# Half of the weight-stream loads issued from ScalarE's queue, and the two stores of x_out released one by one, in a four-sublayer hybrid layer on 8 cores

## The reference

```python
x = x + _L0_attn_a_ref(_layernorm(x), ...)   # S4: causal convolution of length 4096 along the last axis, plus D*u
x = x + _L0_ffn_ref(_layernorm(x), ...)      # (xf * in_scale) @ sign(weight).T * out_scale + bias
x = x + _L0_attn_b_ref(_layernorm(x), ...)   # qkv projection, attention over the 2 sequences, output projection
x = x + _L0_ffn_ref(_layernorm(x), ...)      # the same ffn again
```

## Time and profile before

| | us |
|---|---|
| three runs | 9665.15, 9514.95, 9159.04 (median 9514.95) |
| profiled execution, its own time | 9171.16 |
| span of its slowest core (core 1) | 9169.6 |
| TensorE matmul busy | 5810.7 (63%) |
| TensorE weight loads busy (beside the matmuls) | 2509.5 (27%) |
| VectorE busy | 1786.8 (19%) |
| ScalarE busy | 1271.6 (14%) |
| GpSimd busy | 62.7 (1%) |

### The profile page before, as it was taken

How to read it: one execution, slowest core, us unless ns; L and a number is a source line. 1 busy time by engine, 2 the same in 40 slices (tenths; PEclk the granted TensorE clock), 3 DMA queues, 4 the chain that set the end, 5 groups by cost and what they waited for, 6 DMA issues and landing times.

```text
span 9169.6 us, 74755 instructions; the slowest of 8 cores (9125.0 to 9169.6 us)
## 1 busy us (share of the span) xinstructions
PE 5810.7 (63%) x25740; PEld 2509.5 (27%) x25740; DVE 1786.8 (19%) x3462; ACT 1271.6 (14%) x2520; POOL 62.7 (1%) x108
## 2 busy tenths in 40 slices
PE   2402444566777747775686668774777568767876
PEld 0101111122333323332333233332333223323332
DVE  3212010022211222121202221122112131212112
ACT  0211000011111121111111111112111121111111
POOL 0000000000000000000000000000000000000000
PEclk9855676777788768887787778876887778777887
DMA  1299999955266505663464526650665346452664
GB/s 45 69 263 184 160 154 159 184 155 184 63 211 208 179 37 184 211 187 116 147 220 147 183 74 214 206 171 34 198 211 179 110 147 220 147 183 78 217 213 154
DMA packets 365014, 1468.38 MB, mean 160 GB/s; under 512 B 28056, under 2 KB 28057, under 8 KB 352217
## 3 DMA queue, kind: packets, MB, share of 16 engines
q1 hardware_dynamic: 316874, 1211.72, 42.6%
q0 software_dynamic: 38560, 218.31, 11.9%
q10 hardware_dynamic: 9216, 33.56, 1.3%
HBM read 1480.33 MB, written 151.13 MB: 178 GB/s over the span
## 4 chain that ended last, share of the span: by engine, by line
PE 55%; DVE 17%; DMA 14%; issue 7%; ACT 5%; another core or an unknown queue 1%; DVEq 1%; SPq 0%; ACTq 0%; POOL 0%; POOLq 0%
PE PS L585 42%; PE PS L711 5%; PE PS L665 5%; DMA wbuf<-qkv_bf 4%; DMA wbuf<-ffn_bf 4%; DMA oscbf<-wffnT 3%; DVE actT L669 3%; DVE res L824 2%; DVE tr L822 2%; DVE ln_bf L651 2%; DVE actT L784 1%; ACT qkvsb L844 1%; DVE tr L722 1%; DMA x_out<-res 1%; DMA res<-x_in 1%
## 5 line engine op out<-in xcount | busy, mean ns | idle before, releaser
L585 PE MATMUL PS<-wbuf,actT 128*128 128x512 bf16 x18432 | 4329.2, 397 | 725.1 <-DMA wbuf<-qkv_bf 257.1
L585 PEld LDWEIGHTS PS<-wbuf,actT 128*128 128x128 bf16 x18432 | 1856.8, 101 | 3191.8 <-issue 1235.7
L665 PE MATMUL PS<-ident_sb,ln_bf 128*128 128x128 bf16 x2048 | 474.1, 266 | 1801.6 <-DVE ln_bf L651 1392.5
L665 PEld LDWEIGHTS PS<-ident_sb,ln_bf 128*128 128x128 bf16 x2048 | 208.7, 104 | 2080.5 <-issue 2024.6
L822 DVE TENSOR_TENSOR tr<-PS,oscbf 128x512 f32<-128x512 f32 x256 | 177.0, 691 | 2073.8 <-PE PS L585 2049.8
L602 ACT ACTIVATE ln_bf<-res 128x2048 bf16<-128x2048 f32 x96 | 183.3, 1910 | 2809.4 <-DVE res L824 1304.2
L711 PE MATMUL PS<-ttoep,actT 128*128 128x512 bf16 (+3 forms) x2304 | 491.7, 378 | 99.6 <-DVE res L725 95.1
L674 ACT COPY actT<-PS 128x128 bf16<-128x128 bf16 x1280 | 340.5, 266 | 958.5 <-PE PS L665 958.5
L669 DVE COPY actT<-PS 128x128 bf16<-128x128 bf16 x1280 | 287.5, 225 | 729.1 <-PE PS L665 722.5
L852 DVE TENSOR_TENSOR tr<-qkvsb 128x1024 f32<-128x1024 bf16 x8 | 9.8, 1225 | 1815.5 <-ACT qkvsb L844 1815.5
L844 ACT CAST qkvsb<-PS 128x512 bf16<-128x512 f32 x192 | 112.6, 587 | 1698.6 <-PE PS L585 1683.8
(11 more groups left out here) (159 smaller groups left out, 1417.1 us busy)
## 6 DMA issues: line engine op xcount, KB each, us to landing
wbuf<-ffn_bf SPq DMA_DIRECT2D x512, 1024.0 KB, 8.0
wbuf<-qkv_bf SPq DMA_DIRECT2D x384, 1024.0 KB, 5.7
wbuf<-proj_bf SPq DMA_DIRECT2D x256, 1024.0 KB, 6.8
qkv_bf<-wqkvT POOLq DMA_DIRECT2D x3, 16384.0 KB, 405.8
res<-x_in POOLq DMA_DIRECT2D x16, 2048.0 KB, 12.3
qkvsb<-wffnT POOLq DMA_DIRECT2D x32, 1024.0 KB, 9.9
oscbf<-wffnT POOLq DMA_DIRECT2D x32, 1024.0 KB, 9.7
ffn_bf<-oscbf ACTq DMA_DIRECT2D x64, 512.0 KB, 7.1
```

The costliest lines, as they stand in the source:

```text
L585: e.matmul(psv(bb, g), blocks_actT[bb][:, c * 128:(c + 1) * 128], wbuf[bi][:, cc * COLW + g * 512:cc * COLW + (g + 1) * 512], start=(c == ...
L665: pe_n = pe(lambda e, v=view, sap=src_fn(c): e.transpose(v, sap, ident_sb[:]), inc=True)
```

## The change

Two edits. The loads of `wbuf1` and `wbuf3` are issued by ScalarE instead of SyncE, each with the same waits as before. And the stores of `x_out` no longer both wait for VectorE's last instruction: the store of tile 0 waits for the last instruction of its own epilogue, that of tile 1 for its own.

```diff
-        WQUEUE = ["sync", "sync", "sync", "sync"]
+        WQUEUE = ["sync", "scalar", "sync", "scalar"]
...
         def sub_ffn(T, prestats=False):
+            epi_b = [0, 0]
             for i in (0, 1):
                 stage1_ffn(i)
...
                     if prestats:
                         stats_half(bb, win, s_dve.n)
+                    epi_b[bb] = s_dve.n
+            return epi_b
...
             if SUBLAYERS[3]:
-                sub_ffn(T)
-            P.wait("gpsimd", s_dve, s_dve.n)
+                epi_b = sub_ffn(T)
+            else:
+                epi_b = [s_dve.n, s_dve.n]
             for i in (0, 1):
                 s, r0 = (0, T * 128) if i == 0 else (1, T * 128)
+                P.wait("gpsimd", s_dve, epi_b[i])
                 dma("gpsimd", lambda e, i=i, s=s, r0=r0: e.dma_start(
                     out=x_out.ap()[s, r0:r0 + 128, :], in_=res[i][:]), s_st)
```

## The result

| | before | after |
|---|---|---|
| median of all runs (us) | 9433.4 (16 runs) | 9348.6 (14 runs) |
| lowest, highest | 9154.1, 9665.2 | 9218.5, 9742.9 |
| span of the slowest core, profiled execution | 9169.6 | 9216.9 |
| ratio | | 1.0084, 95% interval 1.0051 to 1.0117 |

The change makes the kernel slower by 0.84%, about 77 us (by the interval, 47 to 107). Seven times of the changed kernel stand behind the ratio: six lie between 9218.5 and 9240.3, and one is 9305.6; without that one the ratio would be 1.0072.

A forecast was written before the change was run, and what follows sets the result against it. TensorE was taken as the bound from T=1 on, with weight loads hidden by prefetch, and loads sharing DMA with casts in T=0. 210 - 95 - 48 = +67 us on 9171 gave 9238 us, range 9120 to 9740.

The forecast's parts named there:

- The sum: Whole kernel: late loads 210, T=0 gain 95 and stores gain 48 us make +67 us on the profiled execution's 9171.
- late loads, per iteration from T=1 on: At pass starts, buffer 1's load waits behind ScalarE's work; 29.5 us per iteration, 210 us lost in all.
- T=0, second queue: In T=0, ScalarE's load queue beside the casts gives loads two of three packet turns; 95 us gained.
- stores, in all: At iteration ends, tile 0's store starts earlier; 6 us for each of 8 iterations, 48 us gained.
- the first ffn's second pass: Statistics stand ahead of buffer 1's load on ScalarE; 8.1 us late, 10.1 with slow matmuls.
- proj's second pass: Statistics stand ahead of buffer 1's load on ScalarE; 7.6 us late, 9.6 with slow matmuls.
- proj's first pass: Starts behind the transposes; a landing of 6.5 us fits in the available 6.7 us, so lateness 0.
- ffn first passes: Twice per iteration, buffer 1's load was to come 3.2 us late at the start of the pass.
- slow matmuls: After each TensorE wait of 7 us or more, matmuls lose another 2.0 us; nothing after short waits.
- the first rival: In T=0, casts keep half the packets because both load queues count as one; +162 us, 9333 us, chance 0.18.
- the two ffn passes: In T=0, with loads sped by the second queue, these passes run from 860 to 1102, before 1275.
- three waits for casts: In T=0: 41 us at the third qkv pass, 21 at proj's first window, 77 at proj's last window.

The follow-up runs named there:

- e1: Kernel before with only the stores released one by one, all loads from SyncE; iterations 983.5 us on the core read, against 989.7 before.
- e2: Kernel before with only buffers 1 and 3 loaded from ScalarE, both stores still behind VectorE's last instruction; ratio to before 1.0145.
- e11: Repeat of e1, only the stores released one by one against the kernel before; ratio 0.9948, interval 0.9913 to 0.9984.
- e3: Changed kernel with the first four loads of every pass issued by SyncE, the other twelve alternating; 9049.3 us, ratio to before 0.988.
- e10: Repeat of e3, the changed kernel with the first four loads of every pass from SyncE; 9038.7 us, ratio to before 0.986.
- e12: Changed kernel with only buffer 3 loaded from ScalarE, buffers 0, 1 and 2 from SyncE; iterations 986.1 us on the core read.
- e4: Changed kernel with ScalarE's loads only in T=0, all loads from SyncE from T=1 on; 9074.6 us, ratio to before near 0.991.

## Why the prediction was right or wrong

**The step that failed is the last: the sum's base.** The sum was +67 us on the profiled execution, a ratio of 1.0073, and 1.0084 was measured; 9238 also lies among the six close times of the changed kernel, 9218.5 to 9240.3. But I wrote 9238 us beside a median of 9515, and set against that median the number reads as 2.9% faster, the opposite of my own sum. I had noted that the median lies 3.7% above and then used this only to widen the range. The median would have been no better base: 9515 x 1.0073 = 9584, and the changed kernel's 14 runs have 9348.6, below the 9433.4 of before although the kernel is slower. The forecast should have been given as a ratio to the same kind of execution. My account of what the change does stands apart from this, and term by term it went as follows.

| term | forecast | measured on the cores read | cores' means |
|---|---|---|---|
| late loads, per iteration from T=1 on | 29.5 | 26.2 (after - e1), 27.6 (e2 - before) | 24.5, 23.8 |
| T=0, second queue | -95 | -62 | -52 (half), -73 (heads on SyncE) |
| stores, in all | -48 | -48 (e11's ratio, -80 to -15) | -5.8 per iteration |
| sum | +67 | +77 (the ratio, 47 to 107) | |

The near hit of the sum is partly luck: the late loads were put some 23 us too high (29.5 x 7 = 207 against 183) and T=0's gain 33 us too high, and these two take most of each other away. The measured terms give 183 - 62 - 48 = +73.

- *Late loads: right in place, high by a tenth in total, and partly by luck in the parts.* The heads of passes are the whole cost (e3, e10), and of these nearly only buffer 1 (e12). Single terms are off. At the first ffn's second pass 4.35 us were waited, not 8.1: ScalarE issues the load while its last instruction still runs, and the load landed in 6 us. At proj's second pass 7.52 came, 7.6 forecast, since the earlier issue was given back by a landing of 7.9 instead of 6.5 us. proj's first pass, put at 0, waits 1.5. The ffn first passes wait 2.3 and 1.3, not 3.2. The iteration's waits were 21.0 where the terms make 3.2 x 2 + 8.1 + 3.4 + 7.6 = 25.5; the rest of the 26.2 is about 5 us of slow matmuls and small waits, where I had 4.
- *T=0: mechanism right, size off by a third.* Three queues share the packets in turn, so the first rival (casts keep half) falls. The mis-sized part is the speed of the stream beside the casts. I had 121 us for each of the two ffn passes; from 837 to about 1149 they took 156 each. The casts ran beside them as I wrote: 5287 packets of q0 in these 312 us, 16.9 per us, where I had 16.5 and the earlier trace rows 20.1. The loads did not: 8535 packets, 1.6 for each cast packet and not 2. And a load is more packets than I took. In the earlier trace rows 30.66 MB are 7946 packets, 3858 bytes each, so a load of 1 MB takes 272 and not 256; by my 10.8 ns this is 17 us for the 96 loads, an estimate. Because the stream was slower, of the three waits for casts that I forecast (41, 21 and 77 us) only the last came, and TensorE stood 21.2 us in it. The DMA engines were full all the way, so the total of DMA work set the end. It came at 1857 - 758 = 1099 us after the first cast's issue, where my rates gave 1851 - 785 = 1066. These 33 us are as much as the miss, and the extra packets are half of them. The other half is open; that q1 moved only 1856 packets where q0 moved 2058 shows that SyncE's queue was at times empty, but no run says what that cost.
- *Stores: right within a wide interval.* One store runs behind the other, x_in's loads leave some 6 us earlier.
- *The Trainium skill's rule* that several issuing engines save only issuing time ("DMA: Bandwidth & Descriptors", "Issuing engines are not separate DMA queues") did not hold in T=0, where a third queue's traffic stands beside: 52 to 73 us. From T=1 on, where no other queue is busy, a second queue gave no time at all (983.5 us by the cores' means both in e4 with one queue and in e3 with two), which is what the rule says. Its other rule, turns by queue and packet, agrees with 2058 to 2025 to 1856.

## What to carry to other kernels

A load issued from a compute engine stands in that engine's program order: what it loses is not the issue time but the prefetch across everything that this engine still has to do, so give the first loads of each stage to an engine that is idle there and share out only the rest. A queue added beside a bulk copy takes turns from it, which helps only until the copy itself is the thing waited for; moving one bulk copy into a stretch with idle DMA engines was worth 126 us of T=0, about twice as much. And make a forecast in the unit in which it will be compared: a ratio of like executions.

## What the runs showed that I had not expected

- A DMA in ScalarE's queue that waits for nothing of the instruction ahead is issued 0.10 us after that instruction starts (4468.29 and 4891.18), not after its 1.91 us. The lateness is thus counted from the last instruction's start.
- Bulk copies at the start delay a chain of small DMAs: by 138 us, for two casts that kept the DMA engines busy until 350.
- The time of the first weight matmul, some 840 us in, differs by 35 us between the cores of one execution of the kernel before, which is nearly half of the effect under study. T=0 measured from it differs by 8 us between the same cores (1361.0 to 1368.5). One core of each kernel is thus not enough to compare them by absolute times.
